# Cross-attention and routed experts on one core: bias addition, third normalised row set and choice of experts in other places of their engines' orders

## What is computed

```python
# 1: cross-attention, 16 heads of 16
h = layernorm(x)
q, k, v = h @ Wq.T + bq, ctx @ Wk.T + bk, ctx @ Wv.T + bv
attn = softmax(q_heads * 16**-0.5 @ k_heads.T)          # 128 x 128 for each batch and head
x = x + (attn @ v_heads) @ Wo.T + bo
# 2: one expert of 32 for each token, hidden size 64
h = layernorm(x)
e = argmax(h @ router_w.T + router_b)
x = x + relu(relu(h @ weights1[e] + bias1[e]) @ weights2[e] + bias2[e])
```

## Time and profile before

| | |
|---|---|
| time, 3 runs | 1257.12, 1258.15, 1260.16 us (median 1258.15) |
| profiled execution | 1255.95 us, span 1254.1 us |
| TensorE busy | 1116.6 us (89%) |
| VectorE busy | 972.5 us (78%) |
| ScalarE busy | 830.9 us (66%) |
| GpSimd busy | 843.4 us (67%) |
| mean granted clock of TensorE | 0.97 |

### The profile page before, as it was taken

How to read it: one execution, slowest core, us unless ns; L and a number is a source line. 1 busy time by engine, 2 the same in 40 slices (tenths; PEclk the granted TensorE clock), 3 DMA queues, 4 the chain that set the end, 5 groups by cost and what they waited for, 6 DMA issues and landing times.

```text
span 1254.1 us, 38330 instructions
## 1 busy us (share of the span) xinstructions
PE 1116.6 (89%) x15015; PEld 864.7 (69%) x15015; DVE 972.5 (78%) x2449; ACT 830.9 (66%) x1892; POOL 843.4 (67%) x1613
## 2 busy tenths in 40 slices
PE   5999999999999999999999999999998519988894
PEld 4677777777777777777777777777776308877783
DVE  4787888888888888888888888888887517766773
ACT  3677777777777777777777777777776306655552
POOL 4444776677777777777677677777755575777776
PEclk9999999999999999999999999999999758999997
DMA  7415222522222222222222222222110126766661
GB/s 249 130 54 120 69 70 70 139 78 81 74 74 74 74 76 76 70 70 70 71 76 70 69 70 70 71 76 70 57 36 25 61 81 203 205 205 205 202 174 24
DMA packets 89233, 120.33 MB, mean 96 GB/s; under 512 B 12177, under 2 KB 71964, under 8 KB 88862
## 3 DMA queue, kind: packets, MB, share of 16 engines
q1 hardware_dynamic: 75230, 84.03, 24.0%
q0 software_dynamic: 13824, 33.85, 7.5%
HBM read 60.61 MB, written 59.31 MB: 96 GB/s over the span
## 4 chain that ended last, share of the span: by engine, by line
PE 44%; DVE 32%; POOL 8%; DMA 6%; issue 6%; ACT 4%; POOLq 0%; SPq 0%; DVEq 0%; ACTq 0%
DVE mx L580 14%; PE pB L809 8%; PE pA L762 8%; PE pB L816 5%; DVE nrm L608 5%; POOL pages L377 4%; PE sc L769 4%; DMA arena<-pages 3%; DVE tr L604 3%; PE sc L970 3%; PE sc L791 3%; DVE row L589 3%; PE m L778 3%; POOL out L409 2%; DMA out<-arena 2%
## 5 line engine op out<-in xcount | busy, mean ns | idle before, releaser
L580 DVE TENSOR_REDUCE mx<-m 128x4 bf16<-128x512 f32 x512 | 324.0, 673 | 55.9 <-PE m L778 55.6
L458 ACT ACTIVATE arena<-sc 128x512 f32<-128x512 f32 x512 | 263.5, 600 | 27.8 <-PE sc L800 19.6
L377 POOL DMA_INDIRECT pages<-row,slot_i x128 | 131.1, 1024 | 109.6 <-ACT xn L442 75.1
L409 POOL DMA_INDIRECT out<-arena x160 | 157.6, 985 | 61.2 <-issue 33.2
L791 PE MATMUL sc<-qk 32*128 32x256 f32 x2048 | 163.0, 394 | 0.3
L816 PE MATMUL pB<-wo_s,aT 128*128 128x256 f32 x512 | 139.6, 395 | 14.4 <-DVE aT L613 14.4
L809 PE MATMUL pB<-arena 128*32 128x128 f32 x4096 | 138.8, 276 | 13.9 <-DVE row L589 0.5
L604 DVE STREAM_TRANSPOSE tr<-pB 128x512 f32<-128x512 f32 x128 | 91.8, 718 | 67.7 <-PE pB L809 66.9
L809 PEld LDWEIGHTS pB<-arena 128*32 128x32 f32 x4096 | 104.2, 110 | 31.7 <-DVE row L589 31.6
L539 ACT ACTIVATE arena<-sc 128x256 f32<-128x256 f32 x160 | 61.3, 383 | 89.3 <-PE sc L961 88.8
L791 PEld LDWEIGHTS sc<-qk 32*128 32x128 f32 x2048 | 112.5, 185 | 0.7 <-ACT arena L462 0.6
(11 more groups left out here) (145 smaller groups left out, 2581.1 us busy)
## 6 DMA issues: line engine op xcount, KB each, us to landing
arena<-pages SPq DMA_DIRECT2D x40, 520.0 KB, 4.0
cT<-ctxT SPq DMA_DIRECT2D x64, 256.0 KB, 3.5
xs<-x_in SPq DMA_DIRECT2D x128, 128.0 KB, 2.1
pages<-empty SPq DMA_DIRECT2D x120, 130.0 KB, 2.6
pages<-empty SPq DMA_DIRECT2D x1, 5200.0 KB, 19.7
out<-arena POOLq DMA_INDIRECT x160
w2s<-w SPq DMA_DIRECT2D x1, 2080.0 KB
qk<-w SPq DMA_DIRECT2D x1, 2064.0 KB, 10.0
```

What stands on the lines that cost most here:

```text
L377: pool.indirect_dma_start(pages, bass.IndirectOffsetOnAxis(slot_i[:, u:u + 1], 0), row[:, q % 4, u, :], None, bounds_check=last_slot, oob_ ...
L409: pool.indirect_dma_start(out_rows, bass.IndirectOffsetOnAxis(pr[:, r, COL_TOKEN:COL_TOKEN + 1].bitcast(U32), 0), pr[:, r, 0:D], None, bou ...
L458: act.activation(pt[:, u % 2, g].rearrange("p i k -> p (i k)"), sc[g][:, :], ACT.Exp).then_inc(S["exp_out"], 1)
L580: ins = dve.tensor_reduce(mx[:, 32 * g:32 * g + 4], mb[i][:, :].rearrange("p (h k) -> p h k", h=4), AX.X, ALU.max)
```

## The change

On GpSimd `add_bo(s+1)` moves from behind `rstd2(s-1, 1)` to behind `slots_as_integers(s-3)`, ahead of the wait for the squares and of `scatter(s-3)`. On ScalarE `norm2(s-1, 2)` moves, within step 2, from ahead of `squares` and `exps` to behind `rank_copy`, next to `norm2(s-1, 3)`. On VectorE `choose(s-2)` moves from the end of step 1, where it followed `best`, to step 2, behind `mxT_copy` and ahead of `normalise`. No instruction is added or removed, and no wait is.

```diff
--- before.py
+++ after.py
@@ -392,13 +392,14 @@
                     split(s + 2)
                 if live(s - 3):
                     slots_as_integers(s - 3)
+                if live(s + 1):
+                    add_bo(s + 1)
+                if live(s - 3):
                     if live(s - 1):
                         after(pool, "sq_out", 4, s - 1, 3)
                     scatter(s - 3)
                 if live(s - 1):
                     rstd2(s - 1, 1)
-                if live(s + 1):
-                    add_bo(s + 1)
                 if live(s - 2):
                     meta(s - 2)
                     fresh_pages(s - 2)
@@ -502,8 +503,8 @@
                             norm1(0, v)
                     if u == 0 and s >= 0 and live(s + 1):
                         norm1(s + 1, 2)
-                    if u in (1, 2) and live(s - 1):
-                        norm2(s - 1, u)
+                    if u == 1 and live(s - 1):
+                        norm2(s - 1, 1)
                     if u == 3 and s >= -1 and live(s + 2):
                         norm1(s + 2, 0)
                     if live(q2):
@@ -523,6 +524,7 @@
                     if u == 0 and s >= 0 and live(s + 1):
                         norm1(s + 1, 3)
                     if u == 2 and live(s - 1):
+                        norm2(s - 1, 2)
                         norm2(s - 1, 3)
                     if u == 3 and s >= -1 and live(s + 2):
                         norm1(s + 2, 1)
@@ -686,6 +688,8 @@
                         mxT_copy(s, u)
                     if u < 2 and live(s + 1):
                         xnT_lo(s + 1, u)
+                    if u == 2 and live(s - 2):
+                        choose(s - 2)
                     if s == 0 and u == 0:
                         output_bias()
                     if live(q1):
@@ -701,7 +705,6 @@
                             slot_sum(s - 3)
                     if u == 1 and live(s - 2):
                         best(s - 2)
-                        choose(s - 2)
                     if u == 2 and live(s + 3):
                         stats1(s + 3, (1, 2))
                     if u == 3:
```

## The result

| | before | after |
|---|---|---|
| median of the runs in one comparison | 1259.16 us | 1226.13 us (1224.97 to 1226.64) |
| ratio | | 0.9744, 95% interval 0.9726 to 0.9762 |
| span of the profiled execution | 1254.1 us | 1223.1 us |
| VectorE busy | 972.5 us | 935.9 us |

A forecast was written before the change was run, and what follows sets the result against it. Bound: in step 2 nrm held by add_bo and norm2 waiting for rstd2, in step 1 choose. Terms 27.0 + 1.5 - 0.5 + 3.2 + 4.8 + 0.2 = 36.2 us less give 1222.0; range 1214 to 1228, chance 0.70.

The forecast's parts named there:

- round 1: Round 1 gets two norm2 behind the exponentials: 0.49 us lost.
- round 2: Where add_bo meets the choice of experts: 3.2 us less, bounds 0.5, if the loading traffic returns, to 3.2.
- rounds 4 to 28: Like rounds, counted from round 3 in the prediction: 22.05 us instead of 23.09, 1.04 us less each.
- rounds 29, 30: They load no statistics, so VectorE is less late: 0.75 us less each, 1.5 in all.
- round 31: Exponentials, ranks, output projection and scores no longer wait behind norm2 for rstd2: 4.8 us less, bounds 3 to 6.
- behind it, to the last scatter: Behind round 31's max_transpose the last rank copy is 0.2 us earlier.
- The 0.3 us for later scatters: On GpSimd, scatters behind the moved add_bo start at 612.3 instead of 612.01, 0.3 us later.
- rival D: In step 1 mxT_copy or xnT_lo stands still behind add_bo: 1.6 us a round, 1267 us; chance 0.04.
- A: In step 0 GpSimd's cast wins against nrm: 0.27 us a round, 1229 us; chance 0.11.
- B: Steps 2 and 3 keep their length through an unseen link: 0.57 us a round, 1238 us; chance 0.09.
- C: A late add_bo makes nrm of step 1 stand still: about 1 us a round, 1249 us; chance 0.03.

The follow-up runs named there:

- e12: The changed kernel with all three moves, run again against the kernel before: 1225.92 us, ratio 0.9738.
- e3: Only the move of choose from step 1 to step 2, against the kernel before: 1261.95 us, ratio 1.0035.
- e13: Moves of add_bo and choose, without that of the third norm2, against the kernel before: 1239.64 us, ratio 0.9864.
- e1: Only the move of add_bo ahead of the scatters, against the kernel before: 1237.88 us, ratio 0.9848.
- e4: All three moves, but the third norm2 between the exponentials and the copy of v, against the kernel before: 1218.12 us, ratio 0.9681.
- e14: Moves of choose and the third norm2, without that of add_bo, against the kernel before: 1257.59 us, ratio 1.0000.
- e10: Changed kernel with SyncE's zero fill of half of w2s two rounds later: 1314.31 us, ratio 1.0041 to the kernel before, on a slower chip.

## Why the prediction was right, and where it was not

The gain at each point, before minus after in us, in the profiled executions:

| | forecast | measured | from the starts of max_transpose |
|---|---|---|---|
| start, to the first one | 0 | -2.9 | 33.64, 36.51 |
| round 1 | -0.5 | -0.5 | |
| round 2 | 3.2 | 1.6 | |
| round 3 | 1.04 | -0.5 | |
| rounds 4 to 28 | 26.0 | 25.7 | 152.1 to 903.8; 154.3 to 880.3 |
| rounds 29, 30 | 1.5 | 1.6 | 962.6; 937.5 |
| round 31 | 4.8 | 4.5 | 987.87; 958.25 |
| behind it, to the last scatter | 0.2 | 0.5 | |
| page stage | 0 | 0.9 | |
| sum | 36.2 | 31.0 | |

Only the like rounds repeat to a tenth of a microsecond. In e12, the changed kernel again, rounds 4 to 28 gave 25.7 us, rounds 2 and 3 together 0.2 and round 31 2.6, so how much the ends give differs from one execution to the next.

- **add_bo ahead of the scatters**: right. Its new place costs nothing, nrm is free. The 0.3 us for later scatters was wrong: the first starts 598.84 - 596.88 = 1.96 us behind step 1's max_transpose, 1.92 in the kernel before. Add_bo ends 0.17 us before the first scatter starts. Nrm took 2.40 to 2.63 us where it began with add_bo or the subtraction, and 0.42 alone; the rule of the Trainium skill (SBUF — State Buffer, Who interferes with whom) on instructions with two SBUF inputs agrees. Beside a small GpSimd instruction the traces don't bear the rule out: in the kernel before, nrm at 628.07 took 0.46 us beside GpSimd's pow of line 291 (628.06, 0.72 us), whose operands are in SBUF too. `mxT_copy` took 0.23 us while add_bo ran, so rival D falls. The prediction read more into that section than it says: the section ties its sentence on copies to conditions on their operands, and mxT_copy reads a PSUM bank. No copy from SBUF stood beside add_bo here, so no run shows that sentence or speaks against it.
- **choose behind mxT_copy**: right, 6.86 to 6.87. That it is worth nothing alone or with add_bo alone was not said; e3 and e13 show it.
- **the third norm2 behind the exponentials**: right in mechanism and size, 7.75 for 7.74, and 7.45 for 7.44. The wait that took the place of the old one is the copy of q.
- **round 2, round 3**: the step that failed is "bounds 0.5, if the loading traffic there returns, to 3.2" and its use of 3.2, and that round 3 was counted as a like round. Round 2 gave 1.6, in the middle of the two bounds, and round 3 -0.5 instead of 1.04; in e12 both together gave 0.2, less than the lower bound for round 2 alone. Where TensorE comes earlier to an instruction that isn't loaded, it waits longer there. The six executions with a stop of 2 us or more (e1, e3, e4, e12, e13, e14) have 9.9 to 13.4 us for that step; the one behind this table, with 1.32 us, has 8.99.
- **start**: not in the sum. GpSimd's first rstd1 instruction took 1.79 us instead of 0.50 while VectorE's low (two SBUF inputs) ran beside it, and the normalised rows came 1.15 us later. TensorE's first projections after them then took 0.63 us where the kernel before had 0.40, though the row of that stretch lists the granted clock at 1.00; that difference I can't explain. The two rows:

```profile
8.36 1.79 POOL L272 TENSOR_SCALAR rs<-ag 128x4 f32<-128x4 f32 x1 [0.30 <-DVE ag L576]
...
8.76 2.01 DVE L649 SCALAR_TENSOR_TENSOR wqkv<-arena,wqkv 128x512 fp32r<-128x512 f32 x3
```

  No edit touches this place. The first max_transpose came at 34.25, 34.82, 33.13, 35.76 and, for the changed kernel again, 35.36 us in other executions, and the changed kernel with the later fill (e10) has 33.92, so the 2.9 us come and go from one execution to the next and are not the change's.
- **round 31**: mis-sized by 0.25. The norm2's wait left the exponentials' way, but the step before it took 7.92 instead of 7.35 us: after 1.51 us of idle TensorE's mean granted clock from 948 to 951 us was 0.59, most of it the lower level of 1.2 GHz, and fourteen scores took 2.02 us instead of 1.08. The kernel before has the same 1.51 us of idle there and kept 1.00 from 973 to 976 us, so the idle time alone doesn't decide it. In e12 the clock was at 0.68 and 0.70 in the first two steps of round 31, which took 7.84 and 8.56 us instead of 6.45 and 7.92; that this term came within 0.3 us of its forecast is in part luck.
- **rivals**: A came once (round 3, step 0) and in no like round; nrm is at 621.46 and the cast at 621.61, 0.15 us apart, as forecast (0.14). B, C and D don't appear in any like round.

## What to carry to other kernels

A wait that hangs on an engine two steps back is a fixed distance; shortening the steps between gives nothing until every such distance is moved. So price edits as a set: here the single effects add up to 23 us and the set gives 32, and one of them is negative alone. Then look for idle time of the engine that becomes the bound and put the moved work there, not beside it. And spread large fills that are not needed soon: one of them probably held up the instruction loads of the busiest engine here, and in four pieces it cost nothing.

## What the runs showed of the hardware

- With the DMA engines 0.87 busy with one 2 MB fill, no packet came on q8, by all signs TensorE's program, between 99.4 and 115.0 us. TensorE stopped for 0.3 to 2.9 us in twelve traces and went on 2.2 to 2.5 us behind the start of the late packet in each. The Trainium skill (SBUF — State Buffer, Who interferes with whom) says that DMA never contends with a compute engine; no run here speaks against that for data, and here it was, as read above, the program that came late.
- One of GpSimd's smallest operations (line 284) grows from 0.23 us to 0.31 to 0.39 beside VectorE's choose, and one at the start from 0.50 to 1.79.
- One chip of the same type ran the kernel before 4% slower (1308.9 us); the four versions traced there had a page stage of 267 us instead of 225 and a late signal beside GpSimd's scatters. The change with the later fill had a ratio of 1.0041 there, where the change gains 2.6% on the usual chips.
